# 4-bit feed-forward stages: up products ahead of down, two block products on GpSimd

## The reference

```python
def fp4_quant_dequant(x):            # blocks of 16 along the last axis
    xb = x.reshape(shape[:-1] + (shape[-1] // 16, 16))
    scale = jnp.max(jnp.abs(xb), axis=-1, keepdims=True) / 6.0
    scale = jnp.maximum(scale, jnp.float32(1e-12))
    xn = xb / scale
    idx = jnp.searchsorted(_MID, jnp.abs(xn))          # grid 0, .5, 1, 1.5, 2, 3, 4, 6
    return (_GRID[idx] * jnp.sign(xn) * scale).reshape(shape)

def fp4_linear(x, w):
    return jnp.einsum('bsk,nk->bsn', fp4_quant_dequant(x), fp4_quant_dequant(w))

gate = fp4_linear(x, w_gate)         # 128 -> 352 features
y = fp4_linear(x, w_up)              # 128 -> 352
h = jax.nn.silu(gate) * y
return fp4_linear(h, w_down)         # 352 -> 128
# x = x + 0.5 * _L3_ffn_ref(_layernorm(x), ...)
```

## Time and profile before

| | |
|---|---|
| median of 3 runs | 5036.86 us (5023.66 to 5044.8) |
| the profiled execution | 5024.43 us, its span 5022.6 us |
| the first of the two 4-bit stages | 3836.16 us to 4069.14 us of the span |
| the second | 4782.66 us to 5014.63 us |
| TensorE, VectorE, ScalarE, GpSimd busy | 81%, 70%, 61%, 31% of the span |

### The profile page before, as it was taken

One profiled execution on the slowest core, in us unless ns is written; L12 is line 12 of the kernel. 1 busy time (PEld: TensorE's weight loads), 2 busy tenths in 40 slices (PEclk: granted clock), 3 DMA queues, 4 the chain that ended last, 5 costly groups with the idle time before them and its releaser, 6 DMA issues.

```text
span 5022.6 us, 66047 instructions
## 1 busy us (share of the span) xinstructions
PE 4048.0 (81%) x15980; PEld 2267.0 (45%) x15980; DVE 3528.2 (70%) x11356; ACT 3069.5 (61%) x5586; POOL 1550.1 (31%) x2846
## 2 busy tenths in 40 slices
PE   4487759999989999998998999983877549999944
PEld 2265633444444444443443444432554436676633
DVE  4588569877777777777777777765657745666576
ACT  1355328888888888888888888881221115565511
POOL 1222124444434444343443443432100023333300
PEclk9678679999999999999999999996998669999976
DMA  1011010000000000000000000000000001111000
GB/s 52 17 32 22 15 21 1 1 20 3 12 12 1 18 5 1 20 3 14 9 1 18 5 6 17 1 1 0 0 0 0 0 22 42 40 40 39 26 0 17
DMA packets 132031, 69.71 MB, mean 14 GB/s; under 512 B 92345, under 2 KB 124814, under 8 KB 129316
## 3 DMA queue, kind: packets, MB, share of 16 engines
q1 hardware_dynamic: 124020, 52.62, 4.3%
q10 hardware_dynamic: 7600, 12.58, 0.7%
HBM read 52.39 MB, written 12.80 MB: 13 GB/s over the span
## 4 chain that ended last, share of the span: by engine, by line
PE 46%; DVE 19%; ACT 15%; issue 11%; POOL 4%; DMA 3%; ACTq 1%; SPq 1%; DVEq 0%; POOLq 0%
PE bank L1805 11%; PE bank L1849 4%; PE bank L1820 4%; PE bank L2574 3%; ACT arena L2034 3%; ACT arena L1909 3%; PE bank L1859 3%; DVE arena L2009 2%; DMA packed_dram<-arena 2%; DVE arena L1986 2%; ACT arena L1897 2%; PE bank L2607 2%; ACT arena L1900 2%; PE bank L643 2%; ACT arena L1896 2%
## 5 line engine op out<-in xcount | busy, mean ns | idle before, releaser
L1805 PE MATMUL bank<-arena 128*128 128x512 f32 x3072 | 1411.0, 596 | 12.1 <-issue 11.8
L1805 PEld LDWEIGHTS bank<-arena 128*128 128x128 f32 x3072 | 588.7, 192 | 761.5 <-issue 749.2
L2046 POOL TENSOR_SCALAR arena<-arena 128x256 f32<-128x256 f32 x1024 | 496.0, 494 | 1215.9 <-DVE arena L1979 1214.8
L1968 DVE SCALAR_TENSOR_TENSOR arena<-arena 128x256 f32<-128x256 f32 x1024 | 393.1, 420 | 303.1 <-ACT arena L1897 303.0
L1820 PE MATMUL bank<-arena 128*128 128x512 f32 x1024 | 537.4, 617 | 39.1 <-DVE arena L2009 38.9
L2009 DVE SCALAR_TENSOR_TENSOR arena<-arena 128x256 f32<-128x256 f32 x1024 | 528.3, 554 | 0.0
L1896 ACT ACTIVATE arena<-bank,bqk 128x512 f32<-128x512 f32 x512 | 351.9, 687 | 221.6 <-PE bank L1805 189.4
L1986 DVE SCALAR_TENSOR_TENSOR arena<-bank,bv,arena 128x256 f32<-128x256 f32 x1024 | 444.7, 472 | 0.0
L1979 DVE SCALAR_TENSOR_TENSOR arena<-bank,bq,arena 128x512 f32<-128x512 f32 x512 | 384.0, 750 | 18.0
L1909 ACT ACTIVATE arena<-arena,const_table 128x512 f32<-128x512 f32 x512 | 374.9, 732 | 0.0
L2585 DVE TENSOR_REDUCE arena<-bank 128x2 f32<-128x512 f32 x256 | 176.2, 688 | 258.5 <-PE bank L2576 258.3
(11 more groups left out here) (371 smaller groups left out, 7577.8 us busy)
## 6 DMA issues: line engine op xcount, KB each, us to landing
arena<-packed_dram SPq DMA_DIRECT2D x48, 192.0 KB
arena<-packed_dram ACTq DMA_DIRECT2D x16, 576.0 KB
arena<-diag_dram SPq DMA_DIRECT2D x16, 256.0 KB, 3.9
arena<-in_L_attn_Wk_dram SPq DMA_DIRECT2D x16, 256.0 KB, 3.2
arena<-in_L_attn_Wq_dram SPq DMA_DIRECT2D x16, 256.0 KB, 4.0
arena<-in_L_attn_Wv_dram SPq DMA_DIRECT2D x16, 256.0 KB, 4.4
arena<-in_L_attn_Wo_dram SPq DMA_DIRECT2D x8, 512.0 KB, 3.8
arena<-in_L_attn_W_dram SPq DMA_DIRECT2D x16, 256.0 KB, 2.7
```

The costliest lines, as they stand in the source:

```text
L1805: nc.tensor.matmul(bank[:, RING1[m % 5], :], w1p[k][:, i * P:(i + 1) * P], zT_of(g), start=True, stop=True).then_inc(a1_proj.sem, 1)
L2046: last = nc.gpsimd.tensor_scalar(a, a, 1.0, a1_ksum[:, i % 4, b:b + 1], ALU.add, ALU.mult)
```

## The change

It makes three changes in the 4-bit stage. In TensorE's list, the gate and up products of group s now stand ahead of the down products of group s - 1, and ScalarE's list follows suit (silu ahead of the copies for down). GpSimd makes the product silu times up for a whole group in one instruction of 128 x 1408 (`gate_pool`); because it can't read PSUM, ScalarE copies the up half to SBUF (`f3_upc`) right after each silu, and this copy, not a VectorE product, now frees the PSUM pair. GpSimd also makes the last of the ten steps on h, the product with the block scales (`scale_h_pool`, L714 with another engine). VectorE keeps nine steps on h. Buffers that two engines now share between groups are doubled, the last step's results are signalled by a semaphore of their own (`f3_hq_done`), and the quantization of x gets its own smaller scratch.

```diff
--- before.py
+++ after.py
@@ -37,7 +37,7 @@
 C_HEAD = C_TINY + 1
 C_ALL = C_HEAD + 16
 
-ARENA = 28320
+ARENA = 28256
 
 
 def host_table():
@@ -692,7 +692,7 @@
         BLOCK = 16
         F3B = [(b * P, min(P, FF3 - b * P)) for b in range(-(-FF3 // P))]
 
-        def fp4_steps(src, dst, scale, inv, v, m, nb):
+        def fp4_steps(src, dst, scale, inv, v, m, nb, eng=nc.vector):
 
 
 
@@ -711,7 +711,7 @@
                 lambda: nc.vector.tensor_scalar(m, m, 1.0, 1.5 * 2.0 ** 22, ALU.max, ALU.mult),
                 lambda: nc.vector.tensor_tensor(v, v, m, ALU.add),
                 lambda: nc.vector.tensor_tensor(v, v, m, ALU.subtract),
-                lambda: nc.vector.tensor_tensor(blocks(dst), blocks(v), spread(scale), ALU.mult),
+                lambda: eng.tensor_tensor(blocks(dst), blocks(v), spread(scale), ALU.mult),
             ]
 
         FP4_STEPS = 10
@@ -732,19 +732,24 @@
                           (wd[:, r0:r0 + rows], [(wdT[0:rows, i, :], None)])]
             f3_scale = scratch("f3_scale", [P, NBH])
             f3_inv = scratch("f3_inv", [P, NBH])
-            f3_v = scratch("f3_v", [P, QT * FF3])
+            f3_v = scratch("f3_v", [P, QT * D])
+            f3_hv = scratch("f3_hv", [P, 2, QT * FF3])
+            f3_hscale = scratch("f3_hscale", [P, 2, NBH])
+            f3_hinv = scratch("f3_hinv", [P, NBH])
             f3_m = scratch("f3_m", [P, QT * FF3])
-            f3_h = scratch("f3_h", [P, QT, FF3])
-            f3_silu = scratch("f3_silu", [P, 2, FF3])
+            f3_h = scratch("f3_h", [P, 2, QT, FF3])
+            f3_silu = scratch("f3_silu", [P, 2, QT, FF3])
+            f3_upc = scratch("f3_upc", [P, 2, QT, FF3])
             f3_xq = scratch("f3_xq", [P, 2, QT, D])
             f3_hq = scratch("f3_hq", [P, 2, QT, FF3])
             f3_hT = scratch("f3_hT", [P, 2, len(F3B), GT])
             f3_wstep = sem("f3_wstep")
             f3_xstep = ev("f3_xstep", per=FP4_STEPS)
-            f3_hstep = ev("f3_hstep", per=FP4_STEPS)
+            f3_hstep = ev("f3_hstep", per=FP4_STEPS - 1, credit=2 * (FP4_STEPS - 1), by="vector")
+            f3_hq_done = ev("f3_hq_done", credit=2, by="gpsimd")
             f3_up = ev("f3_up", per=QT)
-            f3_act = ev("f3_act", per=QT)
-            f3_mul = ev("f3_mul", per=QT, credit=2, by="vector")
+            f3_act = ev("f3_act", per=QT, credit=2, by="scalar")
+            f3_mul = ev("f3_mul", credit=2, by="gpsimd")
             f3_turned = ev("f3_turned", per=len(F3B), credit=2 * len(F3B), by="tensor")
             f3_copied = ev("f3_copied", per=len(F3B), credit=2, by="scalar")
             f3_psum = ev("f3_psum", credit=2, by="tensor")
@@ -790,7 +795,7 @@
                 if n and isinstance(g, int) and g == 0:
                     x_written.wait(nc.tensor, n * G - 1)
                 for q in range(QT):
-                    f3_mul.wait_free(nc.tensor, s, q + 1)
+                    f3_act.wait_free(nc.tensor, s, q + 1)
                     nc.tensor.matmul(bank[:, 2 + 2 * (q % 2), 0:FF3], xT_tile(u, q), wgT[:], start=True, stop=True)
                     nc.tensor.matmul(bank[:, 3 + 2 * (q % 2), 0:FF3], xT_tile(u, q), wuT[:], start=True, stop=True)\
                         .then_inc(f3_up.sem, 1)
@@ -799,30 +804,45 @@
                 s = g + rep * G
                 if n and isinstance(g, int) and g == 0:
                     x_written.wait(nc.scalar, n * G - 1)
+                f3_mul.wait_free(nc.scalar, s)
                 for q in range(QT):
                     f3_up.wait(nc.scalar, s, q + 1)
-                    nc.scalar.activation(f3_silu[:, q % 2, :], bank[:, 2 + 2 * (q % 2), 0:FF3], ACT.Silu)\
+                    nc.scalar.activation(f3_silu[:, u, q, :], bank[:, 2 + 2 * (q % 2), 0:FF3], ACT.Silu)
+                    nc.scalar.activation(f3_upc[:, u, q, :], bank[:, 3 + 2 * (q % 2), 0:FF3], ACT.Copy)\
                         .then_inc(f3_act.sem, 1)
+
+            def gate_pool(g, u):
+                s = g + rep * G
+                f3_act.wait(nc.gpsimd, s)
+                f3_hstep.wait_free(nc.gpsimd, s)
+                apart(nc.gpsimd)
+                nc.gpsimd.tensor_tensor(f3_h[:, u], f3_silu[:, u, :, :], f3_upc[:, u, :, :], ALU.mult)\
+                    .then_inc(f3_mul.sem, 1)
+
+            def h_steps(u, eng):
+                return fp4_steps(f3_h[:, u].rearrange("p q f -> p (q f)"),
+                                 f3_hq[:, u, :, :].rearrange("p q f -> p (q f)"),
+                                 f3_hscale[:, u, :], f3_hinv[:], f3_hv[:, u, :], f3_m[:], NBH, eng)
 
             def quant_h_dve(g, u):
                 s = g + rep * G
-                for q in range(QT):
-                    f3_act.wait(nc.vector, s, q + 1)
-                    nc.vector.tensor_tensor(f3_h[:, q, :], f3_silu[:, q % 2, :], bank[:, 3 + 2 * (q % 2), 0:FF3],
-                                            ALU.mult).then_inc(f3_mul.sem, 1)
                 f3_mul.wait(nc.vector, s)
-                f3_turned.wait_free(nc.vector, s)
-                steps = fp4_steps(f3_h[:].rearrange("p q f -> p (q f)"),
-                                  f3_hq[:, u, :, :].rearrange("p q f -> p (q f)"),
-                                  f3_scale[:], f3_inv[:], f3_v[:], f3_m[:], NBH)
-                for i, step in enumerate(steps):
+                f3_hq_done.wait_free(nc.vector, s)
+                for i, step in enumerate(h_steps(u, nc.vector)[:-1]):
                     step().then_inc(f3_hstep.sem, 1)
                     f3_hstep.wait(nc.vector, s, i + 1)
+
+            def scale_h_pool(g, u):
+                s = g + rep * G
+                f3_hstep.wait(nc.gpsimd, s)
+                f3_turned.wait_free(nc.gpsimd, s)
+                apart(nc.gpsimd)
+                h_steps(u, nc.gpsimd)[-1]().then_inc(f3_hq_done.sem, 1)
 
             def down_pe(g, u):
                 s = g + rep * G
                 t = g + n * G
-                f3_hstep.wait(nc.tensor, s)
+                f3_hq_done.wait(nc.tensor, s)
                 for i, (r0, rows) in enumerate(F3B):
                     f3_copied.wait_free(nc.tensor, s, i + 1)
                     if i == 0:
@@ -854,11 +874,11 @@
 
             programs["vector"].append(lambda e: over_groups(
                 e, [(0, stats_dve), (1, apply_dve), (1, quant_x_dve), (2, quant_h_dve), (3, add_dve)]))
-            programs["gpsimd"].append(lambda e: over_groups(e, [(0, rstd_pool)]))
+            programs["gpsimd"].append(lambda e: over_groups(e, [(0, rstd_pool), (1, gate_pool), (2, scale_h_pool)]))
             programs["tensor"].append(lambda e: over_groups(
-                e, [(0, transpose_pe), (1, down_pe), (0, up_pe)], gate(e, n)))
+                e, [(0, transpose_pe), (0, up_pe), (1, down_pe)], gate(e, n)))
             programs["scalar"].append(lambda e: over_groups(
-                e, [(0, copy_act), (1, copy_h_act), (0, silu_act)], gate(e, n)))
+                e, [(0, copy_act), (0, silu_act), (1, copy_h_act)], gate(e, n)))
 
 
         if "attn2" in used:
```

## The result

The changed kernel took 4952.4 us in the median of four runs (4949.6 to 4961.5), against 5037.6 for the kernel before: a ratio of 0.9834 [0.9806, 0.9862], 85 us or 1.7% faster. The forecast was 4974 with a range of 4940 to 5015. The profiled execution took 4949.55 us, its span 4947.7.

What follows compares the result with a forecast made beforehand. Bound: TensorE and VectorE waiting for each other, 27.57 us a group. Forecast: 39.1 + 6 x 23.9 + 11.5 + 9.75 = 203.8 us a stage, 56.4 less over two; 5024.4 becomes 4968, with half the offset 4974; range 4940 to 5015.

Steps and rivals of the forecast that it cites:

- until the first down: 4-bit stage, its start: first gate and up at low clock, copy, products and nine VectorE steps, 39.1 us.
- six steps: 4-bit stage, between first and last step: down, transposes, up, silu, copy and both GpSimd products in series, 23.9 us each.
- The price of the products: GpSimd's two products of 128 x 1408: 3.3 us each, with ends of 3.1 and 4.16.
- The turn of 1.1 for VectorE between the products: Each step: one turn of VectorE's normalization before GpSimd's second product gets in, 1.1 us.
- rival (b): TensorE's clock rises early in every step, down is faster: 29 us less, 4945 us; chance 0.10.
- (c): TensorE's clock rises late, gate and up products cost more: 55 us more, 5029 us, no change; chance 0.12.
- rival (a): VectorE becomes the bound, 24.8 us a step, 4985 us, or products cost 4.16, 5002 us; chance 0.20.
- The predicted ring: 4-bit stage: down, transposes, copy, up, silu, gate product and scale product in series through TensorE and GpSimd, 23.9 us a step.
- the products are dear: GpSimd's products cost 4.16 us each, making 5002 us; an alternative within the rival of chance 0.20.
- The sign that the prediction named: Profile after: VectorE instructions with two SBUF operands take 3 us and more beside GpSimd's products.
- (d): GpSimd's product waits for a run of VectorE steps, 6.83 us: steps of 30.7 us, 5076 us, slower; chance 0.08.
- the half offset of 6 us: Whole kernel: half of the 12.4 us between median and profiled execution, added to 4968 to give 4974 us.

Runs made afterwards that it cites:

- the order alone: Kernel before with only TensorE's and ScalarE's lists turned round (gate and up ahead of down), VectorE keeping all products; 5006.9 us, ratio 0.9928.
- GpSimd's products alone: Changed kernel with TensorE's and ScalarE's lists in the old order and GpSimd's scale product ahead of its gate product; 5094.8 us, ratio 1.0106 to the kernel before.
- scale ahead of gate: Changed kernel with GpSimd's list turned round: scale product of group g-1 ahead of gate product of group g; 4951.5 us, ratio 0.9838 to the kernel before.
- With fills: Changed kernel plus ten unused TensorE products, each of GpSimd's two products replaced by two constant fills; 4906.3 us, ratio 0.9736 to the kernel before.

## Why the prediction was right, and what it mis-sized

**Direction and chain held.** The chain through both engines opened, down waits for the scale product, gate and up run behind down without a wait. That the order alone gives only part of it was only implied; the parts alone show it.

**The size was short**: 56.4 us for the two stages where 87.6 went. By the second stage's own terms:

| term | forecast | measured |
|---|---|---|
| until the first down | 39.1 | 38.6 |
| six steps | 143.4 (23.9 each) | 131.0 (21.84 each) |
| last step | 11.5 | 10.5 |
| tail | 9.75 | 9.1 |
| stage | 203.8 | 189.2 |

The term that was off is the step, and in it three items of the sum. For the group from 4833.15 to 4854.55, 21.4 us: down 7.96 (forecast 8.84), transposes with their copy 1.37 (1.29), up to the start of the gate product 6.12 (5.98 with handover), gate product 3.11 (3.3), and from its end to the next down 2.84 (4.4 with the turn of 1.1).

- *The price of the products.* 3.3 was taken for both. The gate product took 3.15, inside its bounds and next to the straight line's 3.13. The scale product took 2.59, below the lower bound of 3.1, since I priced it by full rows and the earlier trace rows has only small broadcast ones. "GPSIMD Engine Reference", section "3.1 Elementwise — side-by-side cycle accounting", of the Trainium skill puts about 2.6 cycles an element on a `tensor_tensor` with two inputs, which at its 1.2 GHz makes an estimate of 3.05 us; the full product's 3.15 agrees, and the broadcast one's 2.59 lies below what the page calls the floor.
- *The turn of 1.1 for VectorE between the products* did not come. The second product starts at the end of the first (4830.31 behind 4827.20 + 3.15), and L323 stands until both are done. Only behind a fast down is there a pause, of another kind: the scale product waits for VectorE's ninth step (1.75 us at 4808.08).
- *The clock.* Down ran partly at the high level. TensorE in three stretches (length, busy, granted clock): half speed at down's start, then the rise within down.

```profile
4833.15:4838.00 4.85, 4.17 (x18) 0.50 0.01 3
4838.00:4841.00 3.00, 3.00 (x19) 0.64 0.00 0
4841.00:4847.50 6.50, 5.71 (x23) 1.00 0.00 0
```

Down's products took 2.94 (as at 4902.26) to 5.49 us in seven downs of the stage, 4.51 in the mean: between my forecast and rival (b), and nearer the forecast. (c) did not come: gate and up of this group had 2.4 GHz throughout (1.00, against 0.50 above it).

**Which ring is the bound was named wrong in the main.** Prediction and rival (a) lay within a us of each other, and it is mostly (a)'s mechanism, VectorE's work with its standing, that decides: taking TensorE out of the ring left the step as it was, taking the standing away brought 3.1 to 3.3 us. The predicted ring set only the five steps of twelve behind a slow down, and those were 0.8 us longer in the mean (22.3 against 21.55). That a sum over the wrong ring came within 2.1 us of the step is luck: the two rings happen to be nearly tied. The price that (a) carried, 24.8, was its upper end: it had VectorE stand through all 6.6 us of both products. It stood 3.4, since the products themselves take 5.7, and the last part of L713, the add and the statistics run on beside them. Why "the products are dear" was wrong is the same row: they are cheap. The sign that the prediction named, instructions with two SBUF operands of 3 us and more, was half right: L713 is such a one in some steps (4.45 us), but in the others it is the normalization L323, which reads one, that stands.

(d) did not come. At 4776.95 the gate product starts while L709 runs, and L710 behind it stands (the rows are in the last section): GpSimd got in between two of the nine steps and lost 1.1 us (4.25 for 3.15), not a run of 6.83. The group shown above can't tell, since VectorE's nine steps were over when the last copy ended. That "GpSimd's products alone" has steps of 30.7 us, the figure of (d), is chance: there the price of the products falls on the path because the order is the old one.

**The rest of the span.** The unchanged stages took 12.7 us more in the profiled execution, so its 4949.6 is not the whole gain of the stages; the half offset of 6 us that I added for the median was 2.9.

What stays open: why the rise of the clock fell early in some downs and late in others of one stage, which was worth 0.8 us in five of the twelve steps, and what the copy alone would have given.

## What to carry to other kernels

When engines wait for each other in a circle, look for every place where one frees a buffer of the other: reordering alone moved the wait into the middle of a step, and it was gone in the kernels where a copy on ScalarE and not VectorE's product freed PSUM. A product moved to GpSimd costs twice, its own time and the standing of VectorE beside it, and a busy share hides the second: compare the sum of the plain durations with the busy time. Put beside a GpSimd product what need not stand, and feed that product in pieces so that it starts while the work before it still runs.

## What the runs showed of the hardware that was not expected

- A GpSimd product of 128 x 1408 with an operand broadcast over 16 columns takes 2.59 us, with a full operand 3.15.
- Two GpSimd products queued back to back left no turn to a VectorE instruction that waited: L323 stood through the rest of both, 3.46 us, and in "scale ahead of gate" 3.17 (4.28 less 1.11).
- The standing depends on the form. In the changed kernel a 128 x 1408 tensor-with-scalar step stood beside the gate product (L710), a reduction did not beside the scale product (L705). VectorE in order of time, then GpSimd:

```profile
4778.23 3.72 DVE L710 TENSOR_SCALAR arena<-arena 128x1408 int32<-128x1408 int32 x1
...
4917.74 1.61 DVE L705 TENSOR_REDUCE arena<-arena 128x88 f32<-128x1408 f32 x1
```

```profile
4776.95 4.25 POOL L819 TENSOR_TENSOR arena<-arena 128x1408 f32<-128x1408 f32 x1 [1.98 <-ACT arena L811]
...
4917.30 2.58 POOL L714 TENSOR_TENSOR arena<-arena 128x1408 f32<-128x1408 f32 x1 [1.69 <-DVE arena L713]
```

- Fills stop other forms than products do. With fills, a two-operand step ran at 1.62, but in the same kernel a normalization, which reads one, stood beside them until the last of the four fills ended at 4768.81. It did not always: at 4823.66 the normalization took its plain 1.11 us though the last fill ran until 4824.08, and no run tells why. VectorE, then GpSimd:

```profile
4765.14 3.81 DVE L323 TENSOR_SCALAR xn<-x,meanvar,rstd 128x128 f32<-128x128 f32 x4
```

```profile
4767.40 1.41 POOL L843 MEMSET arena<- 128x1408 f32 x1
```
